# Two causal attentions in one kernel: copies of row maxima from ACT's queue, maxima issued by column count, value copies per group, one mask matmul per bank, spare matmuls

## What is computed

```
x = _layernorm(x + _L0_attn_ref(x, ...)); x = _layernorm(x + _L0_ffn_ref(x, ...))
x = _layernorm(x + _L1_attn_ref(x, ...)); x = _layernorm(x + _L1_ffn_ref(x, ...))
# in both attentions, after the rotary embedding of q and k:
scores = jnp.einsum('bhqd,bhkd->bhqk', q, k) / sqrt(16)
scores = jnp.where(causal, scores, -inf)          # 1024 x 1024 per head
attn = jax.nn.softmax(scores, axis=-1)
y = jnp.einsum('bhqk,bhkd->bhqd', attn, v)
```

## Time and profile before

| | |
|---|---|
| median of 3 runs | 1223.14 us (1223.1 to 1231.58) |
| the profiled execution | 1219.56 us, its span 1217.8 us, mean granted TensorE clock 0.868 |
| PE busy | 993.2 us (82%), 5462 matmuls |
| PE weight loads | 511.4 us (42%) |
| DVE, ACT, POOL busy | 684.9, 482.3, 283.4 us |
| first attention, from first maxima to the first work of the next phase | 150.64 to 526.10 us |
| second attention | 697.10 to 1034.63 us |

### The profile page before, as it was taken

One profiled execution on the slowest core, in us unless ns is written; L12 is line 12 of the kernel. 1 busy time (PEld: TensorE's weight loads), 2 busy tenths in 40 slices (PEclk: granted clock), 3 DMA queues, 4 the chain that ended last, 5 costly groups with the idle time before them and its releaser, 6 DMA issues. The chain is left out here.

```text
span 1217.8 us, 14933 instructions
## 1 busy us (share of the span) xinstructions
PE 993.2 (82%) x5462; PEld 511.4 (42%) x5462; DVE 684.9 (56%) x1177; ACT 482.3 (40%) x750; POOL 283.4 (23%) x545
## 2 busy tenths in 40 slices
PE   7889564976887897888869488888888887979998
PEld 5557511322322232265536322233223322857766
DVE  6875071645654665367557476556656661845554
ACT  4322202533544454622352115435454455246740
POOL 2552041122211212202235311122122212201400
PEclk9989855888988888898789659889898888989999
DMA  8220430111101010020012401010000000032101
GB/s 292 82 92 24 95 111 33 24 31 53 31 24 53 14 28 2 1 87 1 1 38 66 129 14 25 24 34 21 21 28 27 15 1 1 36 130 71 49 19 52
DMA packets 42235, 57.13 MB, mean 47 GB/s; under 512 B 7280, under 2 KB 30384, under 8 KB 41392
## 3 DMA queue, kind: packets, MB, share of 16 engines
q1 hardware_dynamic: 42160, 56.14, 15.5%
HBM read 43.41 MB, written 12.32 MB: 46 GB/s over the span
## 5 line engine op out<-in xcount | busy, mean ns | idle before, releaser
L974 DVE TENSOR_REDUCE mx<-psum 128x1 f32<-128x512 f32 (+3 forms) x640 | 379.7, 634 | 286.4 <-PE psum L845 222.2
L863 PE MATMUL psum<-arena_s 99*128 99x512 bf16 (+3 forms) x768 | 210.6, 362 | 96.7 <-DMA arena_s<-mT 54.1
L927 ACT ACTIVATE arena_p<-psum 128x1024 f32<-128x1024 f32 x192 | 175.1, 954 | 238.0 <-PE psum L863 237.7
L841 PE MATMUL psum<-arena_s 96*128 96x512 bf16 (+3 forms) x768 | 253.0, 372 | 17.2 <-DMA arena_s<-k_parts 12.4
L927 ACT ACTIVATE arena_x<-psum 128x512 f32<-128x512 f32 (+1 forms) x192 | 120.8, 676 | 177.1 <-PE psum L863 177.0
L841 PEld LDWEIGHTS psum<-arena_s 96*128 96x128 bf16 x768 | 77.1, 105 | 173.6 <-DVE mx L974 88.3
L863 PEld LDWEIGHTS psum<-arena_s 99*128 99x128 bf16 x768 | 57.1, 103 | 198.1 <-ACT arena_p L927 67.0
L881 PE MATMUL psum<-arena_p,v_grp 128*32 128x512 f32 (+1 forms) x768 | 111.9, 666 | 27.3 <-POOL arena_p L1021 27.3
L845 PE MATMUL psum<-maskb,ident_b 128*128 128x128 bf16 x512 | 118.1, 249 | 0.0
L257 PE MATMUL psum<-x_h,w 128*128 128x512 f32 x224 | 88.8, 460 | 10.9 <-DVE w L474 7.8
L1021 POOL TENSOR_SCALAR_AFFINE_SELECT arena_p<-arena_p 128x256 f32<-128x256 f32 x128 | 49.7, 406 | 168.1 <-ACT arena_p L927 168.1
(11 more groups left out here) (202 smaller groups left out, 1239.0 us busy)
## 6 DMA issues: line engine op xcount, KB each, us to landing
q_parts<-arena_p SPq DMA_DIRECT2D x48, 128.0 KB
arena_s<-q_parts SPq DMA_DIRECT2D x32, 192.0 KB, 3.0
ff_raw<-in_w_in SPq DMA_DIRECT2D x11, 512.0 KB, 3.5
arena_s<-q_parts SPq DMA_DIRECT2D x32, 128.0 KB, 3.0
k_parts<-arena_p SPq DMA_DIRECT2D x30, 128.0 KB
arena_w<-in_w SPq DMA_DIRECT2D x12, 256.0 KB, 6.3
arena_s<-k_parts SPq DMA_DIRECT2D x8, 384.0 KB
ff_wd_raw<-in_w_down SPq DMA_DIRECT2D x1, 2560.0 KB, 11.9
```

The source lines that it names most:

```text
L841: last = pe.matmul(psum[:, bank, width * n:end], q_st[0:KS, b % NS, 512 * r + P * i:512 * r + P * i + P], k_st[0:KS, g % NS, at:at + width ...
L863: last = pe.matmul(psum[:, 2 * (n % 2) + t, o:512], k_st[0:KM, g % NS, at:at + P], q_st[0:KM, u % NS, 512 * r + o:512 * r + 512], start=Tr ...
L927: act.activation(pr[n % NP_RING][:, :, o:512], psum[:, 2 * (n % 2):2 * (n % 2) + 2, o:512], ACT.Exp, scale=scale).then_inc(exp_ready, 1)
L974: dve.tensor_reduce(mx[:, b % 2, kc, col:col + 4 * len(heads) - 3:4], src, AX, ALU.max)\
```

## The change

- `load_first` loads the queries of units 0 and 1 and the keys of group 0 only; the other first loads and, in layer 0, the load of x come at the start of the attention, x last.
- The copies of maxima are issued by ACT, on its own DMA queue: unit 0's before its exponentials, unit u+1's after the fifth exponential of unit u.
- Entries of the maxima lists are issued by the columns of work done in the unit (5120 in a short unit's list, 13312 in a long one's), one pair of units and 2500 columns ahead. With it lists 0 and 1, the first four entries of list 2, the transposes 0 and 1 and two further entries stand ahead of the first scores. From the formula, the transpose of a long unit's maxima is issued between the last two value visits and the last scores in the long unit before it; that of a short unit's at the end of the short unit before it.
- POOL splits a list's maxima when the formula says that PE has issued the list, two exponentials later: ahead of the last mask of a unit (`b` = 7 in short units, 15 in long ones).
- The two value visits of a loop step stand next to each other; the entries that stood between them come after.
- The mask of a bank with two heads is one matmul of 256 columns instead of two of 128.
- `v_grp` is filled once per group, with all 8 tiles.
- PE runs 16 spare matmuls of 512 columns on the identity ahead of list 0, and one after each entry that stands ahead of the first scores. They write bank 6, whose first real use overwrites it.

```diff
@@ adapter: SP
             stacked.load_first(sp)
-            sp.dma_start(x_tok[:, :, :], d["x"].rearrange("(t p) c -> p t c", p=P))\
-                .then_inc(x_loaded, 16)
@@ StackedOperands.load_first
-        for u in range(NS):
-            self.load_q(sp, u)
-            if u % CH == 0:
-                self.load_k(sp, u // CH)
+        self.load_q(sp, 0)
+        self.load_k(sp, 0)
+        self.load_q(sp, 1)
@@ attention
+    columns = [[0 if what == "T" else what[3] * len(what[1]) for what in x] for x in lists]
+    columns[NU][0] = 2500
+    reached = list(accumulate(n for x in columns for n in x))
+    unit_columns = [sum(x) for x in columns[0:NU]]
+    LEAD = unit_columns[0] + unit_columns[1] + 2500
+    def issued_by(u, slot):
+        done = sum(unit_columns[0:u]) + unit_columns[u] * slot // (4 * n_tiles[steps[u][0]])
+        return sum(1 for n in reached if n <= done + LEAD)
@@ attention: SP
-            def load_max(u):
...
-            for g in range(CH, NS):
+            stacked.load_q(sp, 2)
+            stacked.load_k(sp, 1)
+            stacked.load_q(sp, 3)
+            for g in range(2, NS):
                 stacked.load_k(sp, g)
-            load_max(0)
+            if x_load:
+                sp.dma_start(x_load[0], x_load[1]).then_inc(x_load[2], 16)
             for u in range(NU):
-                if u + 1 < NU:
-                    load_max(u + 1)
...
@@ attention: PE, entry
                 for n, r in enumerate(heads):
...
-                                     k_st[0:KS, g % NS, at:at + width], start=True, stop=kc < c)
-                    if kc == c:
-                        last = pe.matmul(psum[:, bank, end - P:end], ident_b[:, :], maskb[:, :],
-                                         start=False, stop=True)
+                                     k_st[0:KS, g % NS, at:at + width], start=n == 0, stop=kc < c)
+                if kc == c:
+                    n = len(heads)
+                    last = pe.matmul(psum[:, bank, 0:width * n].rearrange("p (h k) -> p h k", h=n)
+                                     [:, :, width - P:width], ident_b[:, :],
+                                     maskb[:, :].rearrange("p (o k) -> p o k", o=1).broadcast_to([P, n, P]),
+                                     start=False, stop=True)
@@ attention: PE, order
+            def spin(count):
+                for _ in range(count):
+                    pe.matmul(psum[:, 6, :], ident_b[:, :],
+                              ident_b[:, :].rearrange("p (o n) -> p o n", o=1).broadcast_to([P, 4, P]),
+                              start=True, stop=True)
+            def maxima(u, slot):
+                nonlocal issued
+                while issued < issued_by(u, slot):
+                    b = next(x for x in range(NU + 1) if issued < first_entry[x + 1])
+                    entry(issued, b, lists[b][issued - first_entry[b]])
+                    issued += 1
+                    if (u, slot) == (0, 0):
+                        spin(1)
+            spin(16)
+            maxima(0, 0)
...
                             scores(au, akt, p)
-                            maxima(4 * n + 2 * k + p + 1)
+                            maxima(u, 4 * n + 2 * (2 * k + p) + 1)
                     values(u, n)
-                    maxima(4 * n + 5)
                     values(u, n + 1)
-                    maxima(4 * n + 7)
+                    maxima(u, 4 * n + 6)
                     if ahead:
                         scores(*ahead[1], 1)
-                    maxima(4 * n + 8)
+                    maxima(u, 4 * n + 8)
@@ attention: ACT
+            def load_max(u):
+                act.wait_ge(qk_taken, turn_entry(u) + 1)
+                act.dma_start(q_st[KS:KM, u % NS, :].rearrange("j (a q) -> j a q", q=P), mT[:, u % 2, :])\
+                    .then_inc(max_loaded[u % NS], 16)
+            load_max(0)
             for u in range(NU):
                 for b in range(2 * n_tiles[steps[u][0]]):
                     exp(u, b)
                     if u and b == 3:
                         copy_o(u - 1)
+                    if u + 1 < NU and b == 4:
+                        load_max(u + 1)
@@ attention: POOL
-            def load_v(u):
+            def load_v(g):
...
+            load_v(0)
+            split = 0
             for u, (c, g) in enumerate(steps):
-                for b in range(8 * c, 8 * c + 8):
+                for b in range(2 * n_tiles[c]):
+                    while split < NU and first_entry[split + 1] <= issued_by(u, max(0, 2 * b - 4)):
+                        split_max(split)
+                        split += 1
+                    if c == 1 and b == 0 and g + 1 < NG:
+                        load_v(g + 1)
+                    if b < 8 * c:
+                        continue
...
-                if u + 2 < NU:
-                    split_max(u + 2)
-                    load_v(u + 2)
```

More of the change, by code:

```diff
@@ L19 @@
 from contextlib import ExitStack
+from itertools import accumulate
 import numpy as np
@@ L198, in build @@
                 wo[0], wo_hl[0])
-        attention(nc, 0, att, stacked, arena_o, arena_p, arena_x, v_tok, v_grp, ident_b, maskb, psum)
+        attention(nc, 0, att, stacked, arena_o, arena_p, arena_x, v_tok, v_grp, ident_b, maskb, psum,
+                  (x_tok[:, :, :], d["x"].rearrange("(t p) c -> p t c", p=P), x_loaded))
         w1_raw = view(v_tok[:, :, :].rearrange("p t c -> p (t c)"), 0, [KC, C + 2 * P])
@@ L718, in load_first @@
     def load_first(self, sp):
-        for u in range(NS):
-            self.load_q(sp, u)
-            if u % CH == 0:
-                self.load_k(sp, u // CH)
+        self.load_q(sp, 0)
+        self.load_k(sp, 0)
+        self.load_q(sp, 1)
 def attention(nc, layer, phase, stacked, arena_o, arena_p, arena_x, v_tok, v_grp, ident_b, maskb,
-              psum):
+              psum, x_load=None):
     q_st, k_st, q_loaded, k_loaded, kr = stacked.q, stacked.k, stacked.q_loaded, stacked.k_loaded, stacked.kr
@@ L814, in _ @@
                 if c == 1 and g + NS < NG:
-                    sp.wait_ge(scores_ready, first_exp[u + 1])
                     stacked.load_k(sp, g + NS)
@@ L838, in entry @@
                 for n, r in enumerate(heads):
-                    end = width * (n + 1)
                     at = T * key_head(r) + 512 * kc
-                    last = pe.matmul(psum[:, bank, width * n:end],
+                    last = pe.matmul(psum[:, bank, width * n:width * n + width],
                                      q_st[0:KS, b % NS, 512 * r + P * i:512 * r + P * i + P],
-                                     k_st[0:KS, g % NS, at:at + width], start=True, stop=kc < c)
-                    if kc == c:
-                        last = pe.matmul(psum[:, bank, end - P:end], ident_b[:, :], maskb[:, :],
-                                         start=False, stop=True)
+                                     k_st[0:KS, g % NS, at:at + width], start=n == 0, stop=kc < c)
[5 more added lines that the diff above has]
+                                     start=False, stop=True)
                 last.then_inc(qk_ready, 1)
@@ L876, in values @@
                 if kt == 0:
-                    pe.wait_ge(vg_ready, u + 1)
+                    pe.wait_ge(vg_ready, u // CH + 1)
                     if u:
@@ L881, in values @@
                     last = pe.matmul(psum[32 * r:32 * r + VW, 6, o:512],
-                                     v_grp[:, u % 2, kt, r if layer == 0 else 0, :],
+                                     v_grp[:, u // CH % 2, kt, r if layer == 0 else 0, :],
                                      pr[(n + r // 2) % NP_RING][:, r % 2, o:512],
@@ L885, in values @@
                 last.then_inc(pv_done, 2)
-            for b in range(2):
-                for n, what in enumerate(lists[b]):
-                    entry(first_entry[b] + n, b, what)
+            def spin(count):
[3 more added lines that the diff above has]
+                              start=True, stop=True)
+            issued = 0
+            def maxima(u, slot):
[8 more added lines that the diff above has]
+            maxima(0, 0)
             for u, kt in blocks[0:2]:
@@ L893, in _ @@
             for u, (c, _) in enumerate(steps):
[L894 to L902, removed]
                 at = blocks.index((u, 0))
@@ L978, in _ @@
         def _(pool):
-            def load_v(u):
[L981 to L986, removed]
+            def load_v(g):
+                if g >= 2:
+                    pool.wait_ge(pv_done, first_exp[CH * g - CH])
+                pool.tensor_copy(v_grp[:, g % 2, :, 0:kr, 0:D],
+                                 v_tok[:, :, vw * g:vw * g + vw]
                                  .rearrange("p t (r f) -> p t r f", f=D)).then_inc(vg_ready, 1)
```

4 lines of the change are left out of this document (removed).

## The result

The changed kernel takes 1106.36 us (median of 4 runs, 1094.72 to 1108.05) against 1223.12 for the kernel before: a ratio of 0.905, 95% interval [0.897, 0.913]. The profiled run took 1094.72, with a span of 1093.0 and a mean granted clock of 0.935 (0.868 before). It is the fastest of them, the other three took 1105.92 to 1108.05: the trace explains the way from 1219.56 to 1094.72, 124.8 us, and what the slower executions lose was not seen.

The account below looks back on a forecast made before the run. PE was taken as busiest, held in both attentions by waits for the copy of maxima, POOL's masking and splitting, and the low clock after. Terms sum to -123.6 from 1219.56, so 1096; forecast median 1098 us, range 1066 to 1142.

Parts of the forecast that it names:

- The pair, sized 34: Steady part of both attentions: a long and a short unit together sum to 33.8 us, taken as 34.
- the visits' 0.8: Value visits on PE: putting two next to each other saves 0.14 each, 0.8 us per pair of units.
- 3 us before it is needed, against 2.3: no wait: Steady pairs: ACT issues the copy of maxima about 3 us before the scores need it, its latency 2.3, so PE never waits.
- rival 3: New queue does not help: copy of maxima still comes out behind the key load; 1133 us, chance 0.08.
- the prediction's own sign of it: On PE, a wait for the copy of maxima that ends with a key load would show the new queue not helping.
- The start: Layer 0's attention up to its first scores: they come at 176.3 instead of 195.91, -19.6 us.
- The spare matmuls: Maxima lists: one per entry hides behind DVE at the upper clock level; 1 us taken per layer, ends 0 and 16.
- rival 2: Spare matmuls don't lift the clock and PE becomes the bound in the lists; 1128 us, chance 0.05.
- Layer 1's start: Loads moved behind -5, sixteen spares +5, list spares +1, transpose 1 ahead of scores +4, unit 0 -5: taken as 0.
- Rivals 1 and 4: Clock still drops once a pair, 1127, chance 0.20; uncovered reduction-to-transpose chain at 30 turns makes it slower, 1297, chance 0.03.
- rival 5: No wait at the last visit and early ends of both starts: 31.7 us a pair, 1064 us, chance 0.05.

## Why the prediction was right, and where two of its steps failed

The median, 1106.4, lies 8 us above the 1098 forecast and well inside the range. That the sum came out is luck: two errors of 20 and 18 us, one in each layer's pairs, cancel. Term by term, from the starts of units above and in the earlier trace rows, so between the two profiled executions, of whose 124.8 us the other 1.5 lie behind the second attention:

| term | forecast | measured |
|---|---|---|
| start of layer 0, to the first scores | -19.6 | -17.2 |
| unit 0 of layer 0 | -5 | -4.0 |
| six pairs of layer 0 | -52 | -31.6 |
| last three units | -6 | -5.0 |
| start of layer 1, with unit 0 | 0 | -5.6 |
| six pairs of layer 1 | -37 | -54.7 |
| last three units | -4 | -5.2 |
| sum | -123.6 | -123.3 |

- **The pair, sized 34, is 31.1** where nothing disturbs it (-54.7 in layer 1). Of the 2.9, 0.5 is POOL's wait (0.82, not 1.3), 0.3 ACT's DMA issue, which hides beside the exponential, 0.2 rounding. The other 1.9 lies in what the sum kept from the earlier trace rows: there PE was busy for 29.7 at full clock, the visits' 0.8 taken off, and idle for 2.6 in small spots; measured are 29.0 and 1.2. The lead fills such spots (32.8 a pair without it). The paired visits' 0.7 is real, but is the price of the POOL wait, so the two were one term.
- **"3 us before it is needed, against 2.3: no wait" failed in four pairs of layer 0**, 24 us in all. That is rival 3's mechanism, priced at 6.6 a pair and measured at 5.2 to 6.7 above 34, given 0.08; the prediction's own sign of it, a wait for the copy that ends with a key load, is there four times. The copy did leave ACT 4.0 us before its scores were due (258.46 and 262.46), but took 11.0 and not 2.3. The step took the 4.5 us of the earlier trace rows for a place in SP's queue; the experiments show a meeting on the DMA engines, which ACT's queue leaves as it is. The Trainium skill's sentence in "DMA: Bandwidth & Descriptors", "Issuing engines are not separate DMA queues", that a second issuing engine saves issue time alone, was right for the steady part. At the start that issue time, which the Trainium skill calls usually small, was 23.57 us on SP for two copies, and ACT's issue brought the first exponential 16.8 us sooner.
- **The start** came nearly as walked: POOL's fills off the path, transpose 0 without a wait, list 0 at 151.05 (149.6 forecast, 150.6 as the late end), scores at 178.70 (176.3).
- **The spare matmuls** were hidden as taken (14.00 us of PE in 14.00, 13.96 of DVE) and lifted the clock, so rival 2 is out; what they buy is too small to measure.
- **Layer 1's start** gained where 0 stood: the wait of ACT fell by 6.8 (5 forecast, on the row below), the sixteen cost 4.98 (5), and unit 0 takes 7.33, 8.3 less than before (-5); of the -5.6 in all that leaves 4.5 for the other terms (5 forecast).

```profile
627.90 0.62 ACT L434 CAST arena_p<-arena_o 128x512 bf16<-128x512 f32 x1 [7.20 <-DMA q_parts<-arena_p]
```

- **Rivals 1 and 4** did not come: the clock is 1.00 through the quiet pairs in spite of the 0.82, and the transposes wait 0.7 us in all. The pair of rival 5, 31.7, was undercut in layer 1, with POOL's wait still there.

## What to carry to other kernels

When a small transfer on the path lands just behind a large one, whatever queue it came from, compare its landing with the large one's issue in several places: a constant time (17.0 and 17.1 us here) means that the small one waits for the large one to land, whenever it was issued itself. From one queue alone this doesn't tell the queue from the DMA engines; here the copy on ACT's queue, as late as on SP's, told. Then the cure is the shape of the large transfer or its time, not another queue. A saving on an engine counts only where no other engine's work becomes due earlier through it: the paired visits saved 0.7 us and gave 0.8 back to POOL's mask. Check the uneven pairs one by one; the twelve pairs average 34.3 and are of 31 and of 40.

## What was not expected of the hardware

A load of 768 KB took 16.7 to 17.6 us as three transfers with an outer repeat and 7.0 to 7.8 us as six without one. A copy of 12 KB took 2.2 us alone and 11.0 beside the slow load. PE stayed at 1.2 GHz through 14.00 us in which it shows as busy for 14.00 (the kernel without spares), where the prediction had reasoned that a stretch without gaps raises the clock; with a spare matmul per entry, in the same 14 us also filled, it stood at 2.4 GHz.
